# Column sums of a gated cross-attention kernel moved from every tile's matmuls to one row per batch, with the front reordered

## The reference

```
fake_quant(x, s, z) = (clip(round(x / s + z), 0, 255) - z) * s
x = x + tanh(g_xattn) * matmul(fake_quant(layernorm(x)), fake_quant(ctx))
x = x + tanh(g_ffn) * ffn(layernorm(x))
ffn(x) = sum over 2 chosen of 16 experts: gate_e * ((silu(x@w1+b1) * (x@w2+b2)) @ w3 + b3)   # 256 wide
       + (silu(x@sw1+sb1) * (x@sw2+sb2)) @ sw3 + sb3                                          # shared, 512 wide
```

## Time and profile before

| what | value |
|---|---|
| time of three runs | 326.26, 326.97, 327.03 us (median 326.97) |
| the profiled execution: time / span | 326.59 / 324.7 us |
| TensorE, busy | 299.0 us, 92% of the span |
| VectorE, ScalarE, GpSimd, busy | 186.0, 104.7, 25.7 us |
| granted TensorE clock | 1.0 of full in every slice |

### The profile page before, as it was taken

How to read it: one execution, slowest core, us unless ns; L and a number is a source line. 1 busy time by engine, 2 the same in 40 slices (tenths; PEclk the granted TensorE clock), 3 DMA queues, 4 the chain that set the end, 5 groups by cost and what they waited for, 6 DMA issues and landing times.

```text
span 324.7 us, 4586 instructions
## 1 busy us (share of the span) xinstructions
PE 299.0 (92%) x1892; PEld 151.5 (47%) x1892; DVE 186.0 (57%) x330; ACT 104.7 (32%) x113; POOL 25.7 (8%) x33
## 2 busy tenths in 40 slices
PE   0369879989999999999999999999999999999995
PEld 0234379964444444644444444444444344444442
DVE  2876897785698863585362565378674542110111
ACT  2888266868682450110343301313111000000000
POOL 2100120110000310000000011110121100000000
PEclk9999999999999999999999999999999999999999
DMA  7999044239960455000697600000000011300111
GB/s 285 415 314 290 1 131 131 63 96 230 308 215 0 91 105 129 2 2 0 182 342 256 219 40 2 0 0 0 2 0 0 4 67 67 129 28 36 67 65 65
DMA packets 34163, 35.55 MB, mean 109 GB/s; under 512 B 16068, under 2 KB 28380, under 8 KB 34012
## 3 DMA queue, kind: packets, MB, share of 16 engines
q1 hardware_dynamic: 34128, 35.23, 34.6%
q10 hardware_dynamic: 12, 0.00, 0.0%
HBM read 27.88 MB, written 4.20 MB: 99 GB/s over the span
## 4 chain that ended last, share of the span: by engine, by line
PE 80%; DVE 8%; SPq 7%; ACT 1%; DMA 1%; issue 1%; POOL 1%; DVEq 0%
PE PS L1312 26%; PE PS L1155 19%; PE PS L1369 19%; PE PS L1190 6%; PE PS L1102 6%; SPq L256 4%; DVE stats L662 2%; DVE areaW L716 2%; PE PS L1109 1%; DMA sbr<-in_L_ffn_sb_dram 1%; SPq L248 1%; DVE X L733 1%; PE PS L1171 1%; DVE wrow L742 1%; PE PS L1197 1%
## 5 line engine op out<-in xcount | busy, mean ns | idle before, releaser
L1155 PE MATMUL PS<-areaT,areaW 128*128 128x512 f16 x288 | 62.6, 379 | 1.4 <-DVE SA L747 1.4
L1155 PEld LDWEIGHTS PS<-areaT,areaW 128*128 128x128 f16 x288 | 28.0, 98 | 34.8 <-DVE SA L747 1.6
L1312 PE MATMUL PS<-areaT,area 128*128 128x512 f16 x192 | 41.6, 379 | 0.0
L1312 PE MATMUL PS<-areaT,areaW 128*128 128x512 f16 x192 | 41.6, 379 | 0.0
L896 DVE SCALAR_TENSOR_TENSOR X<-PS,cf,X 128x512 f32<-128x512 f32 x16 | 12.0, 751 | 47.6 <-PE PS L1369 47.1
L1102 PE MATMUL PS<-area,areaQ 128*128 128x512 f16 x128 | 30.5, 389 | 0.9 <-DVE area L699 0.5
L1312 PEld LDWEIGHTS PS<-areaT,area 128*128 128x128 f16 x192 | 18.8, 98 | 22.7
L1312 PEld LDWEIGHTS PS<-areaT,areaW 128*128 128x128 f16 x192 | 18.8, 98 | 22.7
L662 DVE BATCH_NORM_STATS2 stats<-X 128x6 f32<-128x512 f32 x32 | 20.5, 682 | 4.4 <-DMA X<-in_x_dram 4.2
L1369 PE MATMUL PS<-SW,areaH 128*128 128x512 f16 x96 | 22.0, 379 | 0.0
L1369 PE MATMUL PS<-areaW,QI 128*128 128x512 f16 x96 | 22.0, 379 | 0.0
(11 more groups left out here) (154 smaller groups left out, 335.8 us busy)
## 6 DMA issues: line engine op xcount, KB each, us to landing
ring<-in_L_ffn_sw_dram SPq DMA_DIRECT2D x12, 512.0 KB, 4.7
X<-in_x_dram SPq DMA_DIRECT2D x8, 512.0 KB, 6.1
areaT<-in_ctx_dram SPq DMA_DIRECT2D x8, 512.0 KB, 10.8
ring<-in_ctx_dram SPq DMA_DIRECT2D x8, 512.0 KB, 4.2
ring<-in_L_ffn_ew_dram SPq DMA_DIRECT2D x16, 256.0 KB, 5.6
out_dram<-X SPq DMA_DIRECT2D x7, 512.0 KB, 2.6
ring<-in_L_ffn_ew_dram SPq DMA_DIRECT2D x2, 1024.0 KB, 5.0
areaQ<-gate_dram SPq DMA_DIRECT2D x1, 1024.0 KB, 5.4
```

Of the source, the lines that this page charges most:

```text
L1155: last = mm(PS[:, SU_BANK[half * SC + c] + w, lo:hi], SW[:, wp, 2 * c + w, k, :], XT[:, xp, k, tk], start=(k == 0 and n == 0), stop=(k == ...
L1312: last = mm(PS[:, EU_BANK[u] + w, :], W12S[j][:, wp, k, cs], XT[:, xp, k, b * S:(b + 1) * S], start=(k == 0 and n == 0), stop=(k == KC - 1 ...
```

## The change

- Loads: the context's chunks stand between the x tiles (x0, c0, x1, c1 to c4, x2, c5, c6, x3, c7), and the two bias transfers stand ahead of the ring's weight chunks.
- Batch 0: S2 and C1 are gone. TensorE accumulates onesh x Q2[k] over k in banks 6 and 7 (column_sums(k), 2 matmuls for each of the 8 chunks). VectorE adds that, scaled by cf[:, 10:11], to X of tile 0 (first_tile_row); ScalarE writes it scaled to SBUF (column_row into CROW, which shares the buffer B3b), and GpSimd adds CROW to X of tiles 1 to 3 (add_column_row). Tile 2's products wait for crow_rdy, since they use the same banks.
- Batch 1: S2 stays; 2 matmuls (column_row on TensorE, banks 4 and 5) take the place of 16; ScalarE writes CROW ahead of su_silu(3), and GpSimd adds it to tiles 4 to 7.
- All four copies of the transposed q are VectorE's. Each attend waits for its tile's row.
- ScalarE, VectorE, GpSimd and TensorE lists are reordered in the front; ln_rows writes the f16 rows before the f32 rows.

In the diff, the removed lines of the reordered VectorE and TensorE lists and a few empty lines are left out.

```diff
-            for i in range(TB):
+            def load_tile(i):
                 sp.dma_start(X[:, i, :], x_t[i]).then_inc(x_in[i], 16)
-            for k in range(KC):
+
+            def load_ctx0(k):
                 sp.dma_start(CTX0[:, k, :], ctx_in[0, k * P:(k + 1) * P, :]).then_inc(c0_in[k], 16)
+
+            load_tile(0)
+            load_ctx0(0)
+            load_tile(1)
+            for k in range(1, 5):
+                load_ctx0(k)
+            load_tile(2)
+            load_ctx0(5)
+            load_ctx0(6)
+            load_tile(3)
+            load_ctx0(7)
+            sp.dma_start(sbr[0:SC, :], sb1.rearrange("(c p) -> c p", p=P)).then_inc(sbr_in, 16)
+            sp.dma_start(sbr[SC:2 * SC, :], sb2.rearrange("(c p) -> c p", p=P)).then_inc(sbr_in, 16)
...
-            rstd(2, 2, TB)
-            for i in range(TB):
+            def add_column_row(i):
+
+                pool.wait_ge(crow_rdy, i // TB + 1)
+                nc.gpsimd.tensor_tensor(X[:, i, :], X[:, i, :], CROW[:, :], ALU.add).then_inc(x_row, 1)
+
+            rstd(2, 1, 3)
+            rstd(3, 1, TB)
+            pool.wait_ge(x_int, TB)
+            add_column_row(1)
+            rstd(0, 1, TB + 1)
+            add_column_row(2)
+            rstd(1, 1, TB + 2)
+            add_column_row(3)
+            for i in range(2, TB):
                 rstd(i, 1, TB + i + 1)
             rstd(TB, 2, 2 * TB + 2)
             rstd(TB + 2, 2, 3 * TB)
-            for i in range(TB, NT):
+            pool.wait_ge(x_int, NT)
+            add_column_row(TB)
+            add_column_row(TB + 1)
+            rstd(TB, 1, 3 * TB + 1)
+            add_column_row(TB + 2)
+            rstd(TB + 1, 1, 3 * TB + 2)
+            add_column_row(TB + 3)
+            for i in range(TB + 2, NT):
                 rstd(i, 1, 2 * TB + i + 1)
...
+            def column_row(b):
+
+                pb = CROW_BANK[b]
+                act.wait_ge(crow_done, b + 1)
+                act.wait_ge(row_coef, 1)
+                if b == 0:
+                    act.wait_ge(x0_row, 1)
+                else:
+                    act.wait_ge(x_row, TB - 1)
+                nc.scalar.activation(CROW[:, :].rearrange("p (h n) -> p h n", h=2), PS[:, pb:pb + 2, :], ACT.Copy,
+                                     scale=cf[:, 10:11]).then_inc(crow_rdy, 1)
...
             act.wait_ge(tk_T, 2 * TB)
+            column_row(1)
             su_silu_of(3)
...
+            def first_tile_row():
+                pb = CROW_BANK[0]
+                dve.wait_ge(crow_done, 1)
+                dve.wait_ge(x_int, 1)
+                X0 = X[:, 0, :].rearrange("p (h n) -> p h n", h=2)
+                v.scalar_tensor_tensor(X0, PS[:, pb:pb + 2, :], cf[:, 10:11], X0, ALU.mult, ALU.add).then_inc(x0_row, 1)
             def attend(i):
                 dve.wait_ge(at_done, i + 1)
+                if i == 0:
+                    dve.wait_ge(x0_row, 1)
+                else:
+                    dve.wait_ge(x_row, i)
...
+            first_tile_row()
             evac_q1(3)
+            attend(0)
+            bn(0)
             link(v.tensor_scalar(cf[:, 9:10], sc6[:, 3:4], -1.0, HALF, ALU.mult, ALU.add))
             link(v.tensor_scalar(cf[:, 7:8], cf[:, 4:5], cf[:, 9:10], None, ALU.mult))
             link(v.tensor_scalar(cf[:, 6:7], cf[:, 7:8], cf[:, 8:9], float(D), ALU.mult, ALU.mult))
             row_terms(0)
             shared_biases()
+            coefs(0, 1, None, XS, None)
             attend(1)
             lo_chunk("sw", 0)
             ln2_lo(0)
+            bn(1)
+            lo_chunk("sw", 1)
+            lo_chunk("sw", 2)
             coefs(1, 1, None, XS, None)
+            lo_chunk("sw", 3)
             attend(2)
             bn(2)
             ln2_lo(1)
             coefs(2, 1, None, XS, None)
             attend(3)
+            bn(3)
             ln2_lo(2)
             link(v.tensor_scalar(cf[:, 11:12], cf[:, 1:2], 1.0 / DNS, None, ALU.mult))
             coefs(3, 1, None, XS, None)
+            lo_chunk("sw", 4)
+            ln2_lo(3)
...
+            def column_sums(k):
 
                 for h in range(2):
-                    for n in range(2):
-                        last = mm(PS[:, AT_BANK[i] + h, :], C1[:, n, :], S2[:, h * 512:(h + 1) * 512], start=False,
-                                  stop=(n == 1))
-                last.then_inc(at_done, 1)
+                    last = mm(PS[:, CROW_BANK[0] + h, :], onesh[:, :], Q2[:, k, h * 512:(h + 1) * 512],
+                              start=(k == 0), stop=(k == KC - 1))
+                if k == KC - 1:
+                    last.then_inc(crow_done, 1)
+            def column_row():
+                for h in range(2):
+                    last = mm(PS[:, CROW_BANK[1] + h, :], onesh[:, :], S2[:, h * 512:(h + 1) * 512], start=True, stop=True)
+                last.then_inc(crow_done, 1)
...
             pe.wait_ge(q1_rdy, 3)
+            pe.wait_ge(crow_rdy, 1)
+            for k in range(4):
                 products(2, k)
+            pe.wait_ge(q1_rdy, TB)
+            bias_columns()
+            row_sums(0)
+            for k in range(4, KC):
+                products(2, k)
             pe.wait_ge(r1_rdy, 1)
             pe.wait_ge(sbT_rdy, 2)
+            for k in range(4):
                 products(TB - 1, k)
             transpose_tokens(0)
+            for k in range(4, KC):
+                products(TB - 1, k)
...
-            pe.wait_ge(s2_rdy, 2)
+            pe.wait_ge(s2_rdy, 1)
+            pe.wait_ge(su_hf, 3)
+            column_row()
             for i in range(TB, NT):
                 if i == TB:
                     pe.wait_ge(tk_hi, TB)
                     pe.wait_ge(tk_lo, TB)
                 if i == TB + 1:
                     pe.wait_ge(r1_rdy, B)
-                if i >= TB + 2:
-                    pe.wait_ge(su_hf, i - TB + 1)
+                if i == TB + 2:
+                    pe.wait_ge(crow_rdy, 2)
+                if i == TB + 3:
+                    pe.wait_ge(su_hf, SC)
                 for k in range(KC):
                     products(i, k)
-                column_sums(i)
```

More of the change, by code:

```diff
@@ L95, in build @@
         B3 = [wrow[:, 1, :].bitcast(F32), B3b[:, :]]
+        CROW = B3b
         ebc = sb("ebc", [P, SLOTS + 1, 2, HC], F32)
@@ L486, in ln_rows @@
                 act.wait_ge(coef2, i + 1)
-                if i >= 2:
-                    act.wait_ge(ln_lo, i - 1)
-                nc.scalar.activation(rows[:, i % 2, :], X[:, i, :], ACT.Identity, bias=lnB[:, i:i + 1],
-                                     scale=lnA[:, i:i + 1]).then_inc(ln_xs, 1)
                 if i in (TB, TB + 1):
@@ L496, in ln_rows @@
                                      scale=lnA[:, i:i + 1]).then_inc(ln_hi, 1)
-            def evac_q1(i):
-                act.wait_ge(q1_T, i + 1)
-                nc.scalar.activation(Q1T[:, i, :, :], bank16(2 + i % 2), ACT.Copy).then_inc(q1_rdy, 1)
+                if i >= 2:
+                    act.wait_ge(ln_lo, i - 1)
+                nc.scalar.activation(rows[:, i % 2, :], X[:, i, :], ACT.Identity, bias=lnB[:, i:i + 1],
+                                     scale=lnA[:, i:i + 1]).then_inc(ln_xs, 1)
+            def column_row(b):
[8 more added lines that the diff above has]
+                                     scale=cf[:, 10:11]).then_inc(crow_rdy, 1)
             def tk_hi_evac(i):
@@ L527, in _ @@
             act.wait_ge(tanh_rdy, 2)
+            quant_ctx(0, 0)
             quant_x(0)
-            quant_ctx(0, 0)
+            quant_ctx(0, 1)
             quant_x(1)
-            evac_q1(0)
-            quant_ctx(0, 1)
-            evac_q1(1)
+            for k in range(2, 6):
+                quant_ctx(0, k)
             quant_x(2)
-            quant_ctx(0, 2)
+            quant_ctx(0, 6)
+            quant_ctx(0, 7)
             quant_x(3)
-            for k in range(3, KC):
-                quant_ctx(0, k)
+            column_row(0)
             for c in range(4):
@@ L912, in _ @@
             clamp_x(0)
             coefs(1, 1, cf[:, 3:4], None, sc6[:, 1:2])
+            evac_q1(0)
+            clamp_ctx(0, 1)
+            clamp_x(1)
+            link(v.tensor_scalar(cf[:, 8:9], sc6[:, 1:2], -1.0, HALF, ALU.mult, ALU.add))
+            clamp_ctx(0, 2)
+            evac_q1(1)
             dve.wait_ge(x_in[2], 16)
             bn(2)
-            clamp_ctx(0, 0)
-            clamp_x(1)
+            clamp_ctx(0, 3)
+            clamp_ctx(0, 4)
+            coefs(2, 1, cf[:, 3:4], None, sc6[:, 1:2])
@@ L918, in _ @@
+            dve.wait_ge(tanh_rdy, 2)
+            link(v.tensor_scalar(cf[:, 4:5], cf[:, 0:1], sc6[:, 0:1], sc6[:, 2:3], ALU.mult, ALU.mult))
+            v.tensor_scalar(cf[:, 10:11], cf[:, 4:5], cf[:, 8:9], None, ALU.mult).then_inc(row_coef, 1)
+            dve.wait_ge(row_coef, 1)
+            clamp_ctx(0, 5)
             dve.wait_ge(x_in[3], 16)
             bn(3)
-            clamp_ctx(0, 1)
-            coefs(2, 2, cf[:, 3:4], None, sc6[:, 1:2])
```

(1 more changed line is left out.)

96 lines of the change are left out of this document (39 added, 57 removed).

## The result

The changed kernel takes 336.62 us (median of four runs, 335.93 to 337.37); the kernel before, run beside it, 327.0 (326.26 to 327.79). The ratio is 1.029, with a 95% interval of 1.026 to 1.033: the change costs 9.6 us. The forecast of 333.5 had the direction and, as will be seen, the place, but was 3.1 us short. Its own range ended at 334.7, the one for 8 cases in 10 at 335.2.

What follows compares the result with a forecast made beforehand. VectorE's chain up to shared_up at 70.20 us, then TensorE, with a barely hidden wait for sd_evac(0), was taken to bound it. 326.6 + 6.5 = 333.1, median 333.5 us; own range 332.3 to 334.7, 8 in 10 322.0 to 335.2.

Steps and rivals of the forecast that it cites:

- The port: GpSimd's adds of 2.3 us hold VectorE steps with two SBUF inputs for the rest of the add; chance 0.48.
- The chain of batch 1: VectorE from S2 at 92.3 through held steps to attend(4) at 103.95 and sd_evac(0) at 130.4, done at 131.7 us.
- The front's loss of its gain: Batch 0 up to shared_up: held adds give back the whole gain; shared_up 0.15 us later than 70.20, 3.5 earlier if free.
- TensorE's matmuls: 512-column matmuls at 0.216 us each: batch 0 loses 16 and gets 16, nothing; batch 1 has 14 fewer, 3.0 us less.
- The wait of shared_down(3): TensorE in batch 1 waits for sd_evac(0), done at 131.7 instead of passing at 125.2: 6.5 us later.
- The sum: Whole kernel: 326.6 us for the profiled execution plus 6.5 gives 333.1; the median, 0.4 above, is 333.5 us.
- Behind it all is TensorE's, unchanged: After shared_down(3)'s wait for sd_evac(0), TensorE's remaining work was taken to last as long as before.
- the rival of 323.0: GpSimd's adds don't hold VectorE; shared_down(3) waits from 118.5 to 121.2 us; 4.0 us gained; chance 0.32.
- Holds only where the add comes upon long steps: lnB escapes behind rstd; holds remain at coefs(1) and adds 4 and 5; 1.0 us later, 328.0; chance 0.13.
- The wait for sd_evac(0) doesn't bind: At shared_down(3): with VectorE's batch 1 and port free of cost, TensorE keeps 3.0 + 3.5 us: 320.5; chance 0.02.

Runs made afterwards that it cites:

- r1: Changed kernel with a single tile's lnB computed from one SBUF tensor, lnA as per-partition scalar: 332.21 us, ratio 1.015.
- s1: Changed kernel with VectorE's sd_evac(0) moved ahead of ln2_lo(7): 333.26 us, ratio 1.018.
- s3: Kernel before with only batch 1's part of the change (column_row on TensorE and ScalarE, four GpSimd adds): 335.21 us, ratio 1.024.
- s2: Changed kernel with batch 1 as before the change, so the new front alone: 328.84 us, ratio 1.003.
- t1: s4 with 34 matmuls of 128 columns put ahead of TensorE's first transposes: 320.69 us, ratio 0.979.
- r4: Changed kernel with 36 matmuls of 512 columns into an unread bank, ahead of TensorE's wait for sd_evac(0): 333.23 us, ratio 1.020.
- r2: Changed kernel with GpSimd's adds to tiles 2, 3, 6 and 7 waiting for coefs of tile i-2: 330.09 us, ratio 1.009.
- r3: Changed kernel with GpSimd's add cut to one column, all waits and order kept: 325.25 us, ratio 0.994.
- s4: Changed kernel with adds 2, 3, 6, 7 behind coefs, add 5 behind the last lo_chunk, sd_evac(0) ahead of ln2_lo(7): 323.10 us, ratio 0.984.

## Why the forecast was right in its direction and short in its size

**The port: right.** The forecast took the hold as the rest of the add, without a row that showed it, from turns seen the other way round; it gave this case 0.48, so being right here was a choice that came out and not a reading. lnB behind rstd is held in all four places named (coefs(0), (1), (4), (5)), for 1.5 to 2.0 us, lo_chunk behind add(4) too. The add takes 2.36 us where 2.3 was taken. The section "SBUF: two separate sides" of "SBUF — State Buffer" in the Trainium skill has it as an exclusive lock that lasts the whole instruction; the trace now agrees in this direction as well, 2.13 us against 0.16. Its condition, two inputs in SBUF, agrees with r1 (0.21 us) and with the attends (1.27).

**The chain of batch 1: right.** The forecast had 11.65 us from S2 to attend(4), 26.45 from there to sd_evac(0), and the wait of shared_down(3) behind it. Measured from column_row's matmuls at 93.61: 11.49 and 26.19. Add(5) came in between lo_chunk and su_low, as put (su_low 2.85). s1, s3 and r1 each shift sd_evac(0), and the end goes with it.

**The front's loss of its gain: right as a sum from crow_rdy on, in part by luck, and wrong before it.** From CROW ready to shared_up the forecast had 43.3 us (27.05 to 70.35), and 42.95 were measured (28.65 to 71.60). That match has luck in it. TensorE's slow products at 38.44 ran inside the time in which attend(2) was late anyway, and the wait for attend(2) was then followed by a block at full rate. s1 and s2 have the same front up to here; their CROW was ready at 27.58 and 27.89, but the block behind attend(2) was slow (3.59 and 3.18 us against 1.96), and from CROW to shared_up they took 43.95 and 43.94 us. Their shared_up, at 71.53 and 71.83, came no earlier than the 71.60 here: a late CROW and a slow block cost about the same there, and either puts shared_up more than 1 us behind the forecast.

Behind both stands the rate of TensorE's matmuls. In the changed kernel's profile CROW was 1.6 us later than forecast. The step that failed is in "TensorE's matmuls": "Batch 0 loses 16 in column_sums and gets 16 (8 chunks by 2): nothing", with 0.216 us each. Six of the new 16 run at 0.43 each, about the rate that TensorE had at a granted clock of 0.50 (8 matmuls in 3.28 us from 132.70), and four of these, with four products, stand ahead of x1's transposes in the new order; VectorE waits 1.87 us for those:

```profile
16.78 0.69 DVE L734 COPY areaQ<-PS 128x1024 f16<-128x1024 f16 x1 [1.87 <-PE PS L1155]
```

They were moved to a place with half the rate. t1 shows it by taking the slow stretch away: CROW at 26.61, 0.4 ahead of the forecast. How long the stretch lasts differs between executions of the same front: in r1 to r4, s1 and s2 CROW was ready at 27.38 to 28.63, so the 28.65 of the changed kernel's profile is at the late end, and the miss is 0.3 to 1.6 us. The rows of before held this, eight products in 3.22 us, and the forecast priced matmuls by a row at 95.85 us. The page "TensorE: Matmul & The Clock Gate" of the Trainium skill, section "Part 1: The HAM clock gate", says that a kernel's first matmuls run at the lower level and that the point of the change differs from run to run; the durations agree, with 14.4 us in r2 and 17.4 in the changed kernel, though the column of the granted clock doesn't show it (last section).

**The wait of shared_down(3): right in place, short in price.** The sum counted the idle time of TensorE and took what follows as unchanged: "Behind it all is TensorE's, unchanged". That is the term that was missing. The clock falls during the wait and the 24 matmuls behind it take 7.42 us instead of 5.35, 2.1 us more in the trace; r4, which fills the wait and leaves it in place, gets 5.35. With 1.0 us from the front (132.72 against 131.7) and 2.1 from the clock, less 0.35 by which what follows shared_down(3) was shorter for a reason that no run here looked for, the forecast's 333.1 for the profiled execution becomes 335.8; 335.93 was measured. It is also what the rival of 323.0 lacked: it had a wait of 2.7 us at the same place (118.5 to 121.2), r3 had one of 2.69, and paid 1.7 us for it. Both failed steps are one: the forecast priced every matmul of 512 columns at 0.216 us, wherever it stood.

**The other rivals.** "Holds only where the add comes upon long steps" falls with the lnB rows. "The wait for sd_evac(0) doesn't bind" falls with s1.

**Open.** After the same idle time of 2.35 us ahead of first_blocks(0)'s second block, r2 ran it in 1.96 us, s4 in 3.01, r3 in 3.12 and t1 in 3.38. What decides between them isn't shown by these runs; the price of a wait of this length is 0 or some 1.0 to 1.4 us. Nor is it shown why r4 gained 1.3 us more than its 24 matmuls have. Nor was it tried to keep add(4) off lo_chunk, which costs 0.8 us of VectorE in s4.
